# Combining expert outputs: gathered rows against an accumulating scatter into the residual in DRAM

## The chip, the cores and the metric

One core of a Trainium2 chip (trn2) runs the whole program. The metric is the device time of one execution in microseconds; the time of a kernel is the median over its runs.

## The reference

The input `x` is 4 x 512 tokens of width 256. Four sublayers are added to it in turn, each scaled by the tanh of a gate:

1. an attention-free block with a banded position bias (`_aft_local`) and a feed-forward part,
2. a mixture of experts: eight experts with two 256 x 256 matrices and a squared relu between them, beside a shared expert of width 512; each token goes to its best two of eight,
3. slot attention with a GRU cell, three iterations,
4. a mixture of experts with gate, up and down matrices (256 x 512, 512 x 256) and biases, again two of eight.

For both mixtures the part that matters here is

```python
# first:  out[token] += weight * expert_e(x[token]) for the two chosen e
binned = jnp.zeros((E, cap, Cc), x.dtype).at[sorted_e, local_pos].set(x[sorted_tok])
inter = jnp.square(jax.nn.relu(jnp.einsum('ecd,efd->ecf', binned, w1_stack)))
outb = jnp.einsum('ecf,edf->ecd', inter, w2_stack)
flat_out = outb[sorted_e, local_pos] * sorted_w[:, None]
moe_out = jnp.zeros((t, Cc), x.dtype).at[sorted_tok].add(flat_out)
# second: y = sum_e probs[n, e] * ((silu(x g_e + gb_e) * (x u_e + ub_e)) d_e + db_e)
y = jnp.einsum('ne,ned->nd', probs, expert_out)
```

## The kernel before, in words

All five engines run a program of their own; semaphores order them. The work has four parts. **A** (the first block, the shared expert and the first routing) and **C** (slot attention and the second routing) run over four batches of 512 tokens in pairs; in which order each engine takes their stages is written out by hand in `ORDER_A` and `ORDER_C`. Behind each stands an **expert loop**, `moe_*(…, m)` with m = 0 and 1, and behind that a **combination**.

*Routing.* `choose` picks two experts for each token and the two factors (`share`), `place` a row for each in the table `routed` in DRAM, and `scatter` (GpSimd, L770) writes the normalised rows there by indirect DMA, eight issues per batch of 512 tokens. `table_dve` turns the counts into a table: which groups of 256 rows belong to which expert, and where they begin. `fill` (L394, on SP) writes zero rows behind the last row of each expert: three ahead of the first group (`first_group_in`, L399), five behind its load. `table_dve` ends with the source row of every token in `outputs` (L633 to L644).

*Expert loop.* For each expert e, each engine reads its first and last group from the table (`bounds`) and loops over them, 19 groups in the first and 21 in the second part. For group t: SP loads `xg` two groups ahead (L392); TensorE turns it (L554), ScalarE copies the high halves `xt` (L469), DVE subtracts to get the low halves (L502). A product of two f32r pairs is three matmuls (L194 to L196), called `product`. TensorE makes the up products, 12 or 48 matmuls, turns the group after next, and makes the down products into two banks, 12 or 24 matmuls. ScalarE and DVE work between them on parts of 128 hidden units. DVE evicts the result to `y` (L540, or L542 with the bias), and SP stores it to `outputs` (L429).

*Weights of the experts.* `raw` is one buffer, `split` two. SP loads the plain weights of the next expert to `raw` (`raw_in`, L374). GpSimd loads the high halves by a casting DMA once expert e - 2 is done (`weights_hi`, L441), and subtracts to get the low halves (`weights_lo`, L449). The first low halves of the second part are DVE's. The attention weights of part C are loaded by SP in the loop of expert 2 (`attention_weights`), with casting loads by GpSimd (L454).

*Combination.* GpSimd waits until all of `y` has landed (`moe_end`) and gathers two rows for each token from `outputs` (L830), eight indirect DMAs per batch. DVE's `combine` (L1266) adds them with their factors to the residual, eight instructions per batch. Behind the first loop, in part C, the first pair of batches is combined before its slots are normalised and the second pair in the first iteration of the first; GpSimd makes the low halves of the GRU weights (L853, L854) behind the first two gathers. Behind the second loop all four batches are combined one after the other, and SP stores them to `out` (L732).

## Time and profile before

| | us |
|---|---|
| median of 3 runs | 1438.11 (1436.95 to 1443.64) |
| the profiled execution | 1434.66 |
| its span, first to last instruction | 1432.9 |
| TensorE busy in it | 1089.3 (76%) |
| DVE busy | 751.5 (52%) |
| ScalarE busy | 387.9 (27%) |
| GpSimd busy | 365.4 (26%) |
| bytes moved | 114.66 MB |

The profile is one execution; its time lies 3.45 us under the median. Engines are called PE (TensorE), PEld (its weight loads), DVE, ACT (ScalarE), POOL (GpSimd) and SP (SyncE, which only issues DMAs). Busy time is no bound by itself here, since the four parts follow one another and each has a different engine in front. Part A lasts until about 400 us, the first expert loop until 524, part C until about 1154, the second loop until 1380.

### The profile page before, as it was taken

How to read it: one execution, taken by the hardware profiler on the slowest of the kernel's cores; microseconds unless marked ns; L12 is line 12 of the kernel's file. 1: busy time of each engine (PE TensorE's matmuls, PEld its weight loads, DVE VectorE, ACT ScalarE, POOL GpSimd, SP SyncE). 2: the span in 40 equal slices, each digit the busy share in tenths (PEclk: the TensorE clock that was granted, in tenths of full speed). 3: DMA queues.
4: the chain of work that ended last, by engine and by line, in shares of the span. 5: the costliest groups of instructions: out<-in, count | busy, mean ns of one | idle time of the engine just before them, and what ended most of it. 6: DMA issues, size and time to landing. Idle time of an engine off the chain costs nothing.

```text
span 1432.9 us, 16450 instructions
## 1 busy us (share of the span) xinstructions
PE 1089.3 (76%) x5562; PEld 896.5 (63%) x5562; DVE 751.5 (52%) x1774; ACT 387.9 (27%) x705; POOL 365.4 (26%) x294
## 2 busy tenths in 40 slices
PE   1987989788756763778999857989897159999940
PEld 0646766476555653566877646868685058998840
DVE  5467555566533446455555553454535536665643
ACT  1204122031122332224242232332422023333320
POOL 4204044041411235411010132010101433224235
PEclk9999989899867896799999968989999569999975
DMA  7700023000257652100000010000000664636435
GB/s 261 240 1 30 1 66 126 1 0 0 74 163 216 179 185 65 43 16 0 1 0 0 15 52 22 0 1 1 0 1 1 196 185 141 191 111 204 145 97 169
DMA packets 92431, 114.66 MB, mean 80 GB/s; under 512 B 6608, under 2 KB 77776, under 8 KB 92240
## 3 DMA queue, kind: packets, MB, share of 16 engines
q1 hardware_dynamic: 72480, 78.46, 16.8%
q0 software_dynamic: 19888, 35.40, 8.6%
q8 instruction: 34, 0.56, 0.2%
q14 instruction: 29, 0.24, 0.1%
HBM read 77.14 MB, written 36.70 MB: 79 GB/s over the span
## 4 chain that ended last, share of the span: by engine, by line
PE 46%; issue 18%; DVE 15%; POOL 5%; DMA 5%; ACT 5%; SPq 3%; another core or an unknown queue 0%; DVEq 0%; POOLq 0%; ACTq 0%
PE PS L194 11%; PE PS L196 10%; PE PS L195 10%; PE PS L1586 7%; DMA xg<-routed 3%; PE PS L1502 2%; POOL routed L770 2%; POOL HB L830 2%; PE PS L1477 1%; POOL rstd L763 1%; DVE SM L1319 1%; PE PS L1398 1%; PE PS L1569 1%; PE PS L1525 1%; ACT HB L992 1%
## 5 line engine op out<-in xcount | busy, mean ns | idle before, releaser
L763 POOL TENSOR_TENSOR rstd<-ve,minus_half 128x4 f32<-128x4 f32 x40 | 40.6, 1016 | 411.9 <-DVE ve L1052 251.2
L194 PE MATMUL PS<-xt,split 128*128 128x256 f32 x412 | 123.4, 300 | 15.4 <-issue 12.3
L195 PE MATMUL PS<-xt,split 128*128 128x256 f32 x412 | 121.4, 295 | 0.0
L196 PE MATMUL PS<-xt,split 128*128 128x256 f32 x412 | 121.2, 294 | 0.0
L1586 PE MATMUL PS<-VP,HB 128*128 128x257 f32 x384 | 98.9, 422 | 15.6 <-DVE VP L1331 15.6
L1586 PEld LDWEIGHTS PS<-VP,HB 128*128 128x128 f32 x384 | 81.7, 214 | 34.6 <-DVE VP L1331 20.6
L449 POOL TENSOR_TENSOR split<-raw,split 128x1024 fp32r<-128x1024 f32 (+1 forms) x15 | 66.6, 4442 | 141.7 <-DMA raw<-down_w 74.2
L194 PEld LDWEIGHTS PS<-xt,split 128*128 128x128 f32 x412 | 84.4, 205 | 19.1 <-issue 15.2
L770 POOL DMA_INDIRECT routed<-S,dest x64 | 65.5, 1024 | 100.1 <-DVE dest L1123 82.9
L194 PE MATMUL PS<-split,hs 128*128 128x256 f32 x244 | 79.2, 324 | 11.6 <-DVE hs L509 10.1
L195 PEld LDWEIGHTS PS<-xt,split 128*128 128x128 f32 x412 | 84.3, 205 | 0.0
L196 PEld LDWEIGHTS PS<-xt,split 128*128 128x128 f32 x412 | 84.1, 204 | 0.0
L830 POOL DMA_INDIRECT HB<-outputs,source x64 | 64.6, 1009 | 66.0 <-DMA outputs<-y 47.3
L488 ACT ACTIVATE act<-PS,colv 128x256 f32<-128x256 f32 x84 | 39.8, 474 | 129.2 <-PE PS L196 129.2
L195 PE MATMUL PS<-split,hs 128*128 128x256 f32 x244 | 71.1, 291 | 0.0
L196 PE MATMUL PS<-split,hs 128*128 128x256 f32 x244 | 71.0, 291 | 0.0
L554 PE MATMUL PS<-ident,xg 128*128 128x128 f32 x168 | 28.0, 293 | 55.9 <-DMA xg<-routed 55.9
L524 DVE SCALAR_TENSOR_TENSOR act<-PS,colv,act 128x256 f32<-128x256 f32 x84 | 40.6, 484 | 52.4 <-ACT act L488 48.2
L194 PE MATMUL PS<-HTS,WHH 128*128 128x512 f32 x144 | 61.4, 426 | 8.9 <-DVE RT L1060 8.9
L1398 PE MATMUL PS<-ident,S 128*128 128x128 f32 x208 | 31.3, 300 | 45.7 <-DVE S L1056 45.5
L992 ACT ACTIVATE HB<-PS,SM 128x512 f32<-128x512 f32 x48 | 33.0, 687 | 117.1 <-DVE SM L1321 106.4
L194 PEld LDWEIGHTS PS<-split,hs 128*128 128x128 f32 x244 | 48.1, 197 | 22.2 <-DVE hs L509 22.0
(305 smaller groups left out, 2811.6 us busy)
## 6 DMA issues: line engine op xcount, KB each, us to landing
xg<-routed SPq DMA_DIRECT2D x44, 256.0 KB, 2.8
outputs<-y SPq DMA_DIRECT2D x40, 256.0 KB, 3.0
outputs<-zeros SPq DMA_DIRECT2D x3, 2048.0 KB, 16.1
routed<-zeros SPq DMA_DIRECT2D x20, 256.0 KB, 5.1
raw<-m_w SPq DMA_DIRECT2D x16, 256.0 KB, 5.6
split<-m_w POOLq DMA_DIRECT2D x16, 256.0 KB, 4.4
x_base<-X SPq DMA_DIRECT2D x8, 512.0 KB
raw<-gate_w SPq DMA_DIRECT2D x8, 512.0 KB, 7.4
```

Source lines behind the costliest of these rows:

```text
L194: pe.matmul(out_, a[1], b[0], start=first, stop=False)
L195: pe.matmul(out_, a[0], b[1], start=False, stop=False)
L196: return pe.matmul(out_, a[0], b[0], start=False, stop=last)
L449: eng.tensor_tensor(w.split[e % 2][:, 1], w.raw[:], w.split[e % 2][:, 0].bitcast(F32), ALU.subtract).then_inc(sem(f"m{m}_lo"), 1)
L488: act.activation(w.act[:, f % 2, 0], PS[:, f, 0:G], ACT.Sigmoid, bias=col("gate_b", b)).then_inc(sem(f"m{m}_act"), 1)
L524: dve.scalar_tensor_tensor(out=a[:, 1], in0=PS[:, f, 0:G], scalar=col("gate_b", e * w.fc + f), in1=a[:, 0], op0=ALU.add, op1=ALU.mult).the ...
L763: pool.tensor_tensor(rstd[h][:], ve[h][:], minus_half[:], ALU.pow).then_inc(sem("rstd_ready"), 1)
L770: pool.indirect_dma_start(out=routed[m], out_offset=bass.IndirectOffsetOnAxis(ap=dest[m][:, n, j, kk:kk + 1], axis=0), in_=S2[h][:, j], in ...
L830: pool.indirect_dma_start(out=rows_h[h][:, kk, j], out_offset=None, in_=outputs, in_offset=bass.IndirectOffsetOnAxis(ap=source[:, n, j, kk ...
L992: act.activation(HB[h][:, j], bank(h, j), ACT.Exp, bias=SM[h][:, 1, j:j + 1], scale=1.0 / 16, accum_out=SM[h][:, 2, j:j + 1]).then_inc(sem ...
L1398: ins = pe.transpose(bank(h, k + c)[:, j * P:(j + 1) * P], src[:, j, c * P:(c + 1) * P], ident[:])
L1586: ins = pe.matmul(bank(h, j)[:, 0:D + 1], HB[h][:, m, j * P:(j + 1) * P], VP[h][:, m, 0:D + 1], start=m == 0, stop=m == TT - 1)
```

## The change

- **Rows carry their own target.** A row of `routed` grows from 256 to 265 floats: the token's number and eight factors, zero except for its two experts. `choose` writes them behind the normalised row in `S2` (now `rows_of`), at the price of two more small DVE instructions per batch. `fill` writes rows that point past the tokens, with factors of zero.
- **Expert outputs are added in DRAM.** ScalarE takes the last nine columns of `xg` aside (`keep`, `shift`: two 128x18 copies per group). The eviction multiplies by the factor: in the first loop DVE does it for each half of 128 rows (`y_out`), in the second DVE adds the bias and ScalarE scales both halves in place (`y_biased`, `y_scaled`). GpSimd then casts the 128 row numbers (`to_row`) and issues an indirect DMA with an add (`add_rows`). In the first loop the two halves go to different tensors, `x_base[0]` and a zeroed `x_add`, each with a semaphore of its own. In the second loop both go to `x_base[1]`, and the second half is issued when the first has landed. `y` stays one buffer.
- **No gathers, no `outputs`.** The three zero fills of 2 MB become one, for `x_add`. Part C loads residual and `x_add` and adds them in one DVE instruction per batch. Behind the second loop SP copies `x_base[1]` to `out`, DRAM to DRAM, in four DMAs. `table_dve` loses the source rows.
- **Weights.** `raw` is two buffers (the second lies in `S0` or `HB`), and SP loads two experts ahead. The high halves are made by ScalarE from `raw` (`weights_hi`), except for the first two experts of the first loop. The low halves are DVE's in the first loop and stay GpSimd's in the second.
- **Places.** Two fills stay ahead of the first group, six go to ScalarE's DMA queue (`late_fills`). The attention weights are loaded behind the second `xg` of the first loop, and GpSimd's casting loads of them ahead of the loop.

```diff
-        routed = [nc.dram_tensor(f"routed{m}", (XROWS, D), F32, kind="Internal").ap() for m in range(2)]
-        outputs = nc.dram_tensor("outputs", (NG * G, D), F32, kind="Internal").ap()
+        x_base = [nc.dram_tensor(f"x_base{m}", (B * T + P, D), F32, kind="Internal").ap() for m in range(2)]
+
+        x_add = nc.dram_tensor("x_add", (B * T + P, D), F32, kind="Internal").ap()
+        sums = [(x_base[0], x_add), (x_base[1], x_base[1])]
...
+        def raw_buffer(m, e):
+
+            return e % 2 if m == 1 else int(e >= 2 and e % 2 == 0)
...
+            i = raw_buffer(m, e)
+            used = [f for f in range(e) if raw_buffer(m, f) == i]
+            if used:
+                sp.wait_ge(sem(f"m{m}_lo"), used[-1] + 1)
...
         def first_group_in(sp, m):
             sp.wait_ge(sem(f"m{m}_table"), 1)
-
-            for e in range(3):
-                fill(sp, m, e, "first_filled")
-            sp.wait_ge(sem("first_filled"), 48 * (m + 1))
-            sp.wait_ge(sem("filled"), 16 * (4 + m * (E - 3)))
-            sp.wait_ge(sem("outputs_filled"), 48)
+            for e in range(2):
+                fill(sp, m, e, "filled")
             for h in two:
                 sp.wait_ge(sem(f"scattered{h}"), 16 * 2 * TT * PAIRS * (m + 1))
+            sp.wait_ge(sem("filled"), 16 * (5 + 2 * (m + 1)))
             group_in(sp, m, 0)
-            for e in range(3, E):
-                fill(sp, m, e, "filled")
-
-        def moe_sp(sp, m, more):
-            w = moe[m]
+
+        def late_fills(act, m):
+            for e in range(2, E):
+                fill(act, m, e, "late_filled")
+
+        def moe_sp(sp, m):
             sp.wait_ge(sem(f"m{m}_turned"), 1)
+            sp.wait_ge(sem(f"m{m}_kept"), 1)
             group_in(sp, m, 1)
+            if m == 0:
+                attention_weights(sp)
+            sp.wait_ge(sem("late_filled"), 16 * (E - 2) * (m + 1))
             for e in range(E):
-                if e == 1:
-                    sp.wait_ge(sem("filled"), 16 * (4 + (m + 1) * (E - 3)))
-                if e == (2, 0)[m]:
-                    more(sp)
-                if 1 <= e < E - 1:
-                    raw_in(sp, m, e + 1)
+                if e + 2 < E:
+                    raw_in(sp, m, e + 2)
                 lo, hi = bounds(sp, m, e)
                 with sp.Fori(lo, hi) as t:
                     group_in(sp, m, t + 2)
-                    counted(sp, m)
-                    sp.wait_ge(sem(f"m{m}_y"), t + 2)
-                    sp.dma_start(outputs[bass.ds(t * G, G), :].rearrange("(a p) d -> p a d", p=P), w.y[:]).then_inc(sem(f"m{m}_yout"), 16)
...
+        def weights_hi(act, m, e, done=None):
 
             w = moe[m]
-            if e >= 2:
-
-                done = pool.value_load(table[m][0:1, e - 1:e], min_val=1, max_val=NG - 1)
-                counted(pool, m)
-                pool.wait_ge(sem(f"m{m}_down"), done)
-            for ap, at, n in expert_sources(m, e):
-                pool.dma_start(w.split[e % 2][:, 0, at:at + n].rearrange("p (c o) -> p c o", c=ap.shape[1]), ap).then_inc(sem(f"m{m}_hi{e % 2}"), 16)
+            i = raw_buffer(m, e)
+            if done is not None:
+                counted(act, m)
+                act.wait_ge(sem(f"m{m}_down"), done)
+                act.sem_inc(sem("passed"), 1)
+            act.wait_ge(sem(f"m{m}_raw{i}"), raw_loads(m, e))
+            act.activation(w.split[e % 2][:, 0], w.raw[i], ACT.Copy).then_inc(sem(f"m{m}_whi"), 1)
...
+            def add_rows(t):
+
+                pool.wait_ge(sem(f"m{m}_meta"), t + 1)
+                for a in range(G // P):
+                    pool.wait_ge(sem(f"m{m}_yout{a - a * m}"), 16 * (t + 1) if m == 0 else 32 * t + 16 + 16 * a)
+                    pool.sem_inc(sem("passed"), 1)
+                    pool.tensor_copy(to_row[:, a:a + 1], meta[:, a, 0:1]).then_inc(sem(f"m{m}_to_row"), 1)
+                    pool.wait_ge(sem(f"m{m}_to_row"), 2 * t + 2 + a)
+                    pool.wait_ge(sem(f"m{m}_y"), 2 * t + 2 + a)
+                    pool.sem_inc(sem("passed"), 1)
+                    pool.indirect_dma_start(out=sums[m][a], out_offset=bass.IndirectOffsetOnAxis(ap=to_row[:, a:a + 1], axis=0),
+                                            in_=w.y[:, a], in_offset=None, compute_op=ALU.add).then_inc(sem(f"m{m}_yout{a - a * m}"), 16)
...
+            for a in range(2 - m):
+                pool.dma_start(sums[m][a][B * T:B * T + P], pad[:, 0:D]).then_inc(sem(f"m{m}_yout{a}"), 16)
+            if m == 0:
+                attention_weights_hi(pool)
             pool.wait_ge(sem(f"m{m}_table"), 1)
-            for e in range(2, E):
-                if m == 0 and e == 3:
-                    attention_weights_hi(pool)
-                weights_hi(pool, m, e)
-                weights_lo(pool, m, e)
+            for h in two:
+                pool.wait_ge(sem(f"x_out{h}"), 16 * PAIRS * (m + 1))
+            for e in range(E):
+                if m == 1 and e < E - 1:
+                    if e == 0:
+                        pool.wait_ge(sem("m1_lo"), 1)
+                    weights_lo(pool, m, e + 1)
+                lo, hi = bounds(pool, m, e)
+                with pool.Fori(lo, hi) as t:
+                    counted(pool, m)
+                    add_rows(t)
+            moe_end(pool, m, hi)
...
+            def y_scaled(t, e):
+
+                act.wait_ge(sem("m1_biased"), t + 2)
+                act.wait_ge(sem("m1_meta"), t + 1)
+                for a in range(G // P):
+                    act.activation(w.y[:, a], w.y[:, a], ACT.Copy, scale=meta[:, a, 1 + e:2 + e]).then_inc(sem(f"m{m}_y"), 1)
...
+                if 1 - m <= e < E - 1:
+                    weights_hi(act, m, e + 1, lo if e else None)
...
+                    else:
+                        x_hi(t + 2)
                         h_hi(t, w.fc - 1)
+                        shift(t)
+                        keep(t + 2)
+                        y_scaled(t, e)
...
+            def y_out(t, e):
+
+                dve.wait_ge(sem(f"m{m}_down"), t + 1)
+                dve.wait_ge(sem(f"m{m}_meta"), t + 1)
+                for a in range(G // P):
+                    dve.wait_ge(sem(f"m{m}_yout{a}"), 16 * t + 16)
+                    dve.tensor_scalar(w.y[:, a], PS[:, 5 + a, 0:D], meta[:, a, 1 + e:2 + e], None, ALU.mult).then_inc(sem(f"m{m}_y"), 1)
+
+            def y_biased(t, e):
+
+                dve.wait_ge(sem(f"m{m}_down"), t + 1)
+                dve.wait_ge(sem(f"m{m}_yout0"), 32 * t + 16)
+                dve.tensor_tensor(w.y[:], PS[:, 5:7, 0:D], DB[:, e].unsqueeze(1).to_broadcast([P, G // P, D]),
+                                  ALU.add).then_inc(sem(f"m{m}_biased"), 1)
...
-            def combine(m, n, h):
-
-                x_t = residual(n, h) if m == 0 else X[h]
-                if m == 0 and n >= 2:
-                    dve.wait_ge(sem(f"second_in{h}"), 32)
+            def combine(n, h):
+
+                if n < 2:
+                    dve.wait_ge(sem(f"x_in{h}"), 16 * (PAIRS + 2))
                 else:
-                    dve.wait_ge(sem(f"x_in{h}"), 16 * (PAIRS + 1) + (m and 16 * (n // 2 + 1)))
-                dve.wait_ge(sem(f"rows{h}"), 16 * 2 * TT * (m * PAIRS + n // 2 + 1))
-                for kk in range(2):
-                    for j in range(TT):
-                        ins = dve.scalar_tensor_tensor(out=x_t[:, j], in0=rows_h[h][:, kk, j], scalar=share[m][:, n, j, kk:kk + 1],
-                                                       in1=x_t[:, j], op0=ALU.mult, op1=ALU.add)
-                        if kk == 1 and j == TT - 1:
-                            ins.then_inc(sem("combined"), 1)
-                        elif j == TT - 1:
-                            step(ins)
-                            chained()
+                    dve.wait_ge(sem(f"second_in{h}"), 48)
+                x_t = residual(n, h)
+                dve.tensor_tensor(x_t[:], x_t[:], added[n], ALU.add).then_inc(sem("combined"), 1)
 
...
+            late_fills(act, 0)
...
-            moe_sp(sp, 1, lambda sp: raw_in(sp, 1, 1))
-            for pair in range(PAIRS):
-                for n, h in of_pair[pair]:
-                    if pair:
-                        sp.wait_ge(sem(f"x_out{h}"), 16 * (2 * PAIRS + pair))
-                    sp.dma_start(X[h][:], x_base[1, n].rearrange("(j p) d -> p j d", p=P)).then_inc(sem(f"x_in{h}"), 16)
-                for n, h in of_pair[pair]:
-                    sp.wait_ge(sem("combined"), B + n + 1)
-                    sp.dma_start(out[n].rearrange("(j p) d -> p j d", p=P), X[h][:]).then_inc(sem(f"x_out{h}"), 16)
+            moe_sp(sp, 1)
+            for n in range(B):
+                sp.dma_start(out[n], x_base[1][n * T:(n + 1) * T]).then_inc(sem(f"x_out{n % 2}"), 16)
             for h in two:
                 sp.wait_ge(sem(f"x_out{h}"), 16 * 3 * PAIRS)
```

Three places in the order of the instructions. First GpSimd in the second expert loop, at a change of expert, before (`raw` and `split` are weights, rows of `ISA` and registers are small):

```order
L437 ISA x2
L441 DMA split<-gate_w 128x2x512 [waits m1_down,m1_table]
L441 DMA split<-up_w 128x2x512
L441 DMA split<-down_w 128x4x256
L449 TENSOR_TENSOR split<-raw,split 128x3072 [waits m1_raw,m1_hi0]
```

and now:

```order
L473 TENSOR_TENSOR split<-HB,split 128x3072 [waits m1_lo,x_out1,m1_whi,x_out0,m1_table]
L360 TENSOR_LOAD table
L360 ISA x2
L361 TENSOR_LOAD table
L361 ISA x2
L509 UNCONDITIONAL_BRANCH
L485 REGISTER_ALU [waits m1_table]
L487 ISA [waits m1_meta]
L489 CAST to_row<-meta 128x1 [waits m1_yout0]
L490 ISA
L493 DMA x_base<-y,to_row 2176x256 [waits m1_to_row,m1_y]
```

GpSimd had only the weights of each expert; it now stands in every group, behind the same subtraction. Second, ScalarE in the second loop, from the end of a group over a change of expert to the next group's first sigmoid, now:

```order
L524 ACTIVATE hs<-PS 128x256 [waits m1_h]
L534 REGISTER_ALU
L535 ISA [waits m1_kept]
L537 ACTIVATE meta<-meta_next 128x18 [waits m1_to_row,m1_y]
L527 REGISTER_ALU
L530 ACTIVATE meta_next<-xg 128x18 [waits m1_meta,m1_xg]
L544 ACTIVATE y<-y,meta 128x256 [waits m1_meta,m1_biased]
L544 ACTIVATE y<-y,meta 128x256
...
L462 ACTIVATE split<-raw 128x3072 [waits m1_table,m1_down,m1_raw0]
...
L561 ACTIVATE act<-PS,colv 128x256 [waits m1_up]
```

Before, the sigmoid (L488) followed directly on the copy of `hs` (L474). Third, SP at the very end, before:

```order
L729 DMA X<-x_base 128x4x256 [waits m1_yout]
L729 DMA X<-x_base 128x4x256
L732 DMA out<-X 128x4x256 [waits combined] x2
L729 DMA X<-x_base 128x4x256 [waits x_out0]
L729 DMA X<-x_base 128x4x256 [waits x_out1]
L732 DMA out<-X 128x4x256 [waits combined] x2
```

and now:

```order
L811 DMA out<-x_base 16x8192 [waits m1_yout0]
L811 DMA out<-x_base 16x8192 x3
```

Four copies that wait for the last add alone stand where eight transfers waited for DVE.

## Rows read from the trace of the kernel before

**Rows 1.** The page: the span.

```profile
span 1432.9 us, 16450 instructions
```

**Rows 2.** Order of time behind the second loop (start us, us, engine, line, operation).

```profile
1383.15 1.04 POOL L830 DMA_INDIRECT HB<-outputs,source  x1 [33.83 <-DMA outputs<-y]
...
1423.02 0.95 POOL L830 DMA_INDIRECT HB<-outputs,source  x1 [0.30 <-issue]
...
1426.11 3.38 DVE L1266 SCALAR_TENSOR_TENSOR X<-HB,share,X 128x256 f32<-128x256 f32 x8 [4.68 <-DMA HB<-outputs,source]
...
1421.46 8.43 SPq L732 DMA_DIRECT2D out<-X  x2
```

**Rows 3.** Busy time of each engine in the second expert loop.

```profile
1160.90:1379.20 218.30, 207.23 (x1600) 197.69 (x1600) 136.33 (x295) 78.52 (x192) 60.94 (x25) 0.97 0.48 149
```

**Rows 4.** Order of time at the start of the second loop.

```profile
1145.88 3.35 DVE L449 TENSOR_TENSOR split<-raw,split 128x3072 fp32r<-128x3072 f32 x1
1146.59 3.46 POOL L770 DMA_INDIRECT routed<-S,dest  x1 [0.30 <-issue]
1150.36 0.96 POOL L770 DMA_INDIRECT routed<-S,dest  x1 [0.30 <-issue]
1153.60 0.40 SPq L392 DMA_DIRECT2D xg<-routed  x1
...
1160.92 1.09 PE L554 MATMUL PS<-ident,xg 128*128 128x128 f32 x4 [22.03 <-DMA xg<-routed]
```

**Rows 5.** DVE's evictions in the second loop, in order of time.

```profile
1176.11 0.69 DVE L542 TENSOR_TENSOR y<-PS,DB 128x512 f32<-128x512 f32 x1 [1.18 <-PE PS L196]
1185.70 0.69 DVE L542 TENSOR_TENSOR y<-PS,DB 128x512 f32<-128x512 f32 x1 [1.17 <-PE PS L196]
1196.31 0.69 DVE L542 TENSOR_TENSOR y<-PS,DB 128x512 f32<-128x512 f32 x1 [1.17 <-PE PS L196]
...
1379.20 0.69 DVE L542 TENSOR_TENSOR y<-PS,DB 128x512 f32<-128x512 f32 x1 [1.17 <-PE PS L196]
```

**Rows 6.** Groups by line in the second loop (busy us, mean ns of one).

```profile
L449 POOL TENSOR_TENSOR split<-raw,split 128x3072 fp32r<-128x3072 f32 x7 | 47.7, 6821 | 85.7 <-DMA raw<-down_w 74.2 <-DMA split<-down_w 11.5
...
L527 DVE SCALAR_TENSOR_TENSOR PS<-PS,colv,act 128x256 f32<-128x256 f32 x80 | 39.4, 493 | 2.9
...
L509 DVE TENSOR_TENSOR hs<-PS,hs 128x256 fp32r<-128x256 f32 x80 | 33.1, 414 | 0.0
```

**Rows 7.** Order of time in the first loop: transposes and evictions.

```profile
410.19 1.12 PE L554 MATMUL PS<-ident,xg 128*128 128x128 f32 x4 [4.31 <-DMA xg<-routed]
...
414.00 0.69 DVE L540 COPY y<-PS 128x512 f32<-128x512 f32 x1 [1.34 <-PE PS L196]
...
418.97 0.69 DVE L540 COPY y<-PS 128x512 f32<-128x512 f32 x1 [0.97 <-PE PS L196]
...
444.65 0.69 DVE L540 COPY y<-PS 128x512 f32<-128x512 f32 x1 [1.87 <-PE PS L196]
457.30 0.69 DVE L540 COPY y<-PS 128x512 f32<-128x512 f32 x1 [1.34 <-PE PS L196]
...
524.24 0.69 DVE L540 COPY y<-PS 128x512 f32<-128x512 f32 x1 [0.97 <-PE PS L196]
```

**Rows 8.** ScalarE's copies from SBUF by line (ns min/median/max, first and last start).

```profile
L889 ACT ACTIVATE W<-HB x1: 1482/1482/1482, 11.4 to 11.4; 128x1536 fp32r<-128x1536 f32 x1
...
L485 ACT ACTIVATE hs<-act x38: 416/417/418, 405.1 to 521.6; 128x256 fp32r<-128x256 f32 x38
```

**Rows 9.** Order of time behind the first loop.

```profile
548.24 10.44 DVE L1266 SCALAR_TENSOR_TENSOR X<-HB,share,X 128x256 f32<-128x256 f32 x8
...
553.78 3.42 POOL L854 TENSOR_TENSOR WHH<-HB,WHH 128x1536 fp32r<-128x1536 f32 x1
...
563.42 1.94 PE L1398 MATMUL PS<-ident,S 128*128 128x128 f32 x8 [16.09 <-DVE S L1056]
...
620.05 6.67 DVE L1266 SCALAR_TENSOR_TENSOR XN<-HB,share,XN 128x256 f32<-128x256 f32 x16
```

**Rows 10.** The page: one kind of DMA issue (count, KB each, us to landing).

```profile
outputs<-zeros SPq DMA_DIRECT2D x3, 2048.0 KB, 16.1
```

216 lines of the change are left out of this document (107 added, 109 removed), and 4 rows, old and new, of the table ORDER_C.

## The prediction

> **What bounds the kernel now.** I read the page first, then the two expert loops in order of time, then the stretches behind each of them. The span is 1432.9 us in a run of 1434.66 [rows 1]; no engine bounds it as a whole, so each stage has to be read by itself. The places that the change touches are these.
>
> *Behind the second expert loop (53.7 us).* The last eviction into `y` starts at 1379.20 [rows 5], and everything up to the end, 1432.9, is the combination: the store of `y` has to land, GpSimd issues 32 gathers one behind the other from 1383.15 to 1423.97, DVE starts on the last batch at 1426.11, and its store ends the span [rows 2]. TensorE has nothing to do there. Look at the gap between 1423.97 and 1426.11: 2.14 us from the end of an issue to its reader.
>
> *In the second expert loop (203 us).* From the first `y` to the last there are 20 intervals, 1379.20 - 1176.11 = 203.1 [rows 5]. Within an expert one takes 9.59 us, across a change of expert 10.61. TensorE is busy in 207.2 of the 218.3 us from its first transpose at 1160.92 on, at a granted clock of 0.97 [rows 3]: this stage is bound by TensorE, and the rest follows in its shadow.
>
> *In the first expert loop (110 us).* 18 intervals from 414.00 to 524.24; a good one is 4.97, the one ahead of 457.30 is 12.65 [rows 7]. Here the chain TensorE, ScalarE, DVE decides, and twice a DMA. The second group's transposes also waited 4.31 us for their `xg` [rows 7].
>
> *Behind the first loop.* DVE's combination of two batches is one after the other in its queue: the first piece takes 10.44 us, because one of its instructions stands still while GpSimd subtracts the GRU weights at 553.78, and TensorE waits 16.09 us for what follows [rows 9].
>
> **The part that no row shows: how long an accumulating scatter takes to land.** Call L the time from the end of GpSimd's issue to the reader. The nearest rows: a gather, 2.14 [rows 2]; a plain scatter, ended 1151.32 and followed by its reader at 1153.60, so at most 2.28 [rows 4]. An accumulate must read the old row in DRAM before it writes, so neither is an upper end. I take 3.0, which is the scatter and a third more, since 128 rows are a small transfer and what is added is mostly one more trip; for the bounds I take 2.3 (the read costs nothing) and 4.4 (the gather and the scatter one after the other). The Trainium skill (DMA: Bandwidth & Descriptors, section "Anatomy of one DMA — SWDGE (gpsimd) path") fits a DMA from GpSimd by 2.0 us and its bytes over 436 GB/s, which for 128 KB would be an estimate of 2.3; by that, the sum below would be about 1406. No run here shows yet that an accumulate obeys this fit, and the same skill (Collectives: The Full Stack, section "The bandwidth ceiling: the fold count and why AG ≠ RS ≠ AR") says that an add costs two source reads, which speaks against it.
>
> **The change part by part**, against 1434.66.
>
> 1. *The end.* 32 gathers, four combinations and their stores go. In their place, from the last eviction: 0.69 for the bias (as the old eviction, [rows 5]), 0.42 for ScalarE's scaling of one half (the 128x256 row, [rows 8]), two issues of 0.96 [rows 4], and about 0.8 for the small cast and six handovers (estimated from the 0.3 between neighbouring issues); that is 3.8, and L twice, since in this loop the second half's add waits for the first's. With L = 3 it is 9.8. Then the copy of 2 MB from DRAM to DRAM. The nearest row is a 2 MB store, 16.1 us in a queue of three [rows 10]; alone it should take less, but bytes are both read and written. I take 12 and half a microsecond for its issue; bounds 8 and 20. 9.8 + 12.5 = 22.3 in place of 53.7: **-31** (-36 to -22).
>
> 2. *Second loop, new experts.* The high halves are now made by ScalarE in 128x3072. From 0.417 us at 256 and 1.482 at 1536 [rows 8], a column costs 0.83 ns, so 2.8 us. For six experts this copy waits until the group before has left TensorE, and what is queued behind it on ScalarE is the first sigmoid of the new expert. That sigmoid was due some 2.5 us after the last matmul (12 matmuls of 207.2 / 1600 = 0.13, [rows 3], and the 1.0 by which a change of expert is longer); it now comes at 1.8 (bias and scaling) + 2.8 = 4.6. The sigmoid takes some 0.5, DVE has then 4 x (2 x 0.49 + 0.41) + 0.7, about 6.3 with no pause [rows 5, 6], and TensorE's last six matmuls of 0.13 stand behind it: 12.2 us against 10.61, so 1.6 x 6 = 10, and 2 for the first group and for ScalarE's scaling in each. **+12** (0 if DVE's pauses take it up, 19 if all 2.8 count).
>
> 3. *Second loop, the adds.* A group's adds are a chain of their own: 3.8 + 2L = 9.8 per group, and `y` can't be overwritten before it has ended. GpSimd also makes the low halves, 6.82 us each [rows 6], ahead of the new expert's adds, which I put at 2 more per change. 20 x 9.8 + 12 = 208 is under TensorE's own 203 + 12 = 215, so at L = 3 it costs **0**. The cover is 7 us, and it is gone at L = 3.2: from there each 0.1 of L costs 4 us.
>
> 4. *Start of the second loop.* `xg` was issued at 1153.60 and read at 1160.92, 7.3 us, since fills, casts and the next weights were in flight [rows 4]. Now the late fills leave from ScalarE before, and the casts are gone; the scatters ahead stay, and so does the 3.46 us one beside DVE's 3.35 us subtraction. **-4** (-6 to 0).
>
> 5. *First loop.* The second `xg` is asked for at once, not behind five fills and two stores: -5. But the attention weights (2.25 MB) and their casting loads (1.75 MB), formerly in the middle, now stand ahead of the third `xg`: +6. The stalls that they and the store of `y` made in the middle go: -10.5, of which 7 in the interval of 12.65 [rows 7]. Two halves go to two tensors, so only one landing counts: issue, cast, issue, landing and eviction again, about 1.75 + L = 4.75 for the second half, under 4.97, but the second half is late by a microsecond and DVE stands behind it: 0.5 x 11 = +5.5. ScalarE's and DVE's copies of 128x1024 at six changes: 0.8 each, +5. **+1** (-10 to +15). DVE's subtraction reads two SBUF tensors while GpSimd issues; rows 4 show what that does to an issue, 3.46 in place of 0.96, and I count at most 1.2 us at a change, hidden by its length. The Trainium skill (SBUF — State Buffer, "Who interferes with whom") infers that such an op does not hold up descriptor generation; by it this would be nothing, and the row says otherwise.
>
> 6. *Behind the first loop.* The second halves' add must land, where a plain store was: **+3**. DVE's combination is one addition of 128x1024 per batch, some 1.2 us (a third of the 3.35, [rows 4], and a little that is fixed), and GpSimd's subtractions come long before it: 9 us on the first batch and 2 on the second, less 1 for the extra loads: **-10** (-12 to -4). In the second pair 6.67 us of combination [rows 9] become 2.5 beside TensorE's gates: **-1**.
>
> 7. Six MB of zeros at the start become two: nothing waits for them, **0**. The routing's extra DVE instructions: **0**.
>
> Sum: -31 + 12 + 0 - 4 + 1 + 3 - 10 - 1 = **-30**, 1404.7 for the profiled execution. The median of the three runs is 3.45 above it, so I forecast **1408 us**. A measurement can tell about 0.5%, 7.2 us, from no change.
>
> **The rivals.**
>
> *The adds take over the second loop (slower).* Place: `y` of one group waits for both adds of the group before, one behind the other. At L = 4.2 a group costs 12.2: 20 x 12.2 + 12 - 203 = +53 in place of +12, with 12 more at the end and in the first loop: -30 + 41 + 12 = +23, **1461**. It decides from L = 3.8, where gains and losses cancel. For it: nothing shows L, the chain takes it 42 times in all, and 9.8 against 10.1 is a thin cover. Against: no plain transfer of this size needs over 2.3. Chance 0.18; between L = 3.7 and 3.9 it is no change, 0.1.
>
> *Copies and adds both in the shadow (faster still).* L = 2.3, and DVE's pauses (1.2 us ahead of each eviction, [rows 5]) take up ScalarE's copy: 8 less in the second loop, 5 in the first, 6 at the end: **1389**. For it: TensorE alone is full. Chance 0.12.
>
> *Transfers crowd the start of the first loop.* 8 MB between 392 and 425 push several `xg`, 15 us in place of 6, and routed rows of 1060 bytes land more slowly: **1423**. Chance 0.1. That the change does not do what it says I leave out: the order of instructions shows the gathers gone.
>
> **How the numbers follow.** The forecast (L up to 3.4: 1395 to 1420) has 0.5. Faster: 0.5 + 0.12 + 0.1 = 0.72; same 0.1; slower 0.18. The range goes from the second rival, a little beyond, to L = 4.05 of the first: 1386 to 1452, with some 0.06 left out below and 0.13 above.
>
> **What would show it.** Right: the stretch behind the last eviction near 22 us; intervals of the second loop 9.6 within an expert and 12 across; TensorE's wait behind the first loop near 7 us, not 16. Wrong: evictions in the second loop that wait for a DMA into `x_base` (then L is over 3.2, and the row gives it), intervals that are alike within and across experts, or an end over 30 us, which would be the DRAM copy.

## The result, and the profile after

The changed kernel takes **1460.65 us** (median of 4 runs, 1460.25 to 1464.78) where the kernel before took 1437.63 (4 runs, 1436.95 to 1443.64): a ratio of 1.019, 95% interval 1.016 to 1.023. It is slower by 23 us, where 1408 was forecast. That is nearly the value of the first rival (1461). The rival had the right place, but it got there with L = 4.2 in every group, and most landings took 2.1 to 3.0 us; that its figure fits is in part luck.

From the page of the changed kernel, which answers to [rows 1]: the span, the chain of waits by engine and by line, and two groups of instructions (busy, mean ns | idle before and who ended it).

```profile
span 1459.0 us, 17260 instructions
...
PE 42%; DMA 18%; DVE 18%; issue 9%; POOL 6%; ACT 5%; SPq 1%; DVEq 1%; POOLq 1%; ACTq 0%
...
L201 PE MATMUL PS<-split,hs 128*128 128x256 f32 x244 | 86.0, 352 | 85.7 <-DVE hs L589 85.1
L493 POOL DMA_INDIRECT x_base<-y,to_row x61 | 95.7, 1569 | 99.3 <-DVE y L597 45.9
```

DMA has 18% of the chain, and 12% of the span lies in it as `x_base<-y,to_row`, the landing of an add. An add's issue takes GpSimd 1569 ns; the plain scatter of [rows 4] takes 960. TensorE stands still for 85.7 us ahead of its down products.

I cut both profiled executions by the same points: VectorE's first subtraction into `xt` of each loop, the start of the last group's eviction into `y` in each loop (its first half, where it has two), and the end. The cuts of the kernel before are 402.20, 524.24, 1162.83, 1379.20 and 1432.9, those of the changed kernel 408.71, 550.63, 1171.01, 1438.39 and 1459.0.

| stage | before | changed | difference | forecast |
|---|---|---|---|---|
| part A, up to the first loop | 402.2 | 408.7 | +6.5 | 0 |
| first loop | 122.0 | 141.9 | +19.9 | +1 |
| part C, to the second loop | 638.6 | 620.4 | -18.2 | -12 |
| second loop | 216.4 | 267.4 | +51.0 | +12 |
| end | 53.7 | 20.6 | -33.1 | -31 |

Their sum is +26.1, the difference of the spans. Where the forecast counted on a gain it came, larger than stated. The loss lies in the two loops, and 6.5 us in part A (term 7 below).

The second loop of the changed kernel in the windows (us, then busy time and count of PE, PEld, DVE, ACT and POOL, granted clock, DMA share, GB/s), which answers to [rows 3]:

```profile
1171.01:1438.39 267.38, 218.60 (x1596) 207.23 (x1596) 132.16 (x295) 121.21 (x280) 117.57 (x87) 0.91 0.36 78
```

TensorE was busy in 207 of 218 us [rows 3]; now it is in 219 of 267, and no longer sets the pace of the loop. Who holds it shows in one group inside an expert, from one eviction to the next, in the timeline of the changed kernel (start, us, engine, line; idle before and who ended it), VectorE, ScalarE and GpSimd in turn:

```profile
1297.89 0.69 DVE L603 TENSOR_TENSOR y<-PS,DB 128x512 f32<-128x512 f32 x1 [4.00 <-DMA x_base<-y,to_row]
...
1309.22 0.69 DVE L603 TENSOR_TENSOR y<-PS,DB 128x512 f32<-128x512 f32 x1 [3.64 <-DMA x_base<-y,to_row]
```
```profile
1298.62 0.91 ACT L544 ACTIVATE y<-y,meta 128x256 f32<-128x256 f32 x2 [4.95 <-DVE y L603]
```
```profile
1298.03 0.19 POOL L489 CAST to_row<-meta 128x1 int32<-128x1 f32 x1 [2.60 <-DMA x_base<-y,to_row]
1299.91 1.56 POOL L493 DMA_INDIRECT x_base<-y,to_row  x1 [1.70 <-ACT y L544]
1303.71 0.19 POOL L489 CAST to_row<-meta 128x1 int32<-128x1 f32 x1 [2.24 <-DMA x_base<-y,to_row]
1305.01 1.56 POOL L493 DMA_INDIRECT x_base<-y,to_row  x1 [1.11 <-issue]
```

Read it as a sum. Eviction and the first half's scaling to 1299.08; 0.83 until GpSimd issues; 1.56 of issue, ended 1301.47; landing at 1303.71, 2.24 later; cast 0.19; 1.11 until the next issue; 1.56, ended 1306.57; and the next eviction starts at 1309.22, 2.65 later. Together 11.33 us, with no slack anywhere, against the 9.59 of TensorE [rows 5]. Both landings together are 4.89, so L was 2.45 here; the rest is 6.44, where my sum had 3.8. This is the shortest interval but the first: the 20 of them take 255.1 us, 12.8 on average.

Two things make the others longer. Ahead of the first add of a new expert GpSimd subtracts low halves for 6.8 to 7.4 us. Here VectorE had written `y` at 1206.91, and the add was issued 6.17 us later, where the group above has 2.02; the next eviction came 15.11 us after the one before:

```profile
1204.24 7.41 POOL L473 TENSOR_TENSOR split<-raw,split 128x3072 fp32r<-128x3072 f32 x1
1210.99 0.78 POOL L489 CAST to_row<-meta 128x1 int32<-128x1 f32 x1
1213.08 1.56 POOL L493 DMA_INDIRECT x_base<-y,to_row  x1 [1.31 <-issue]
```

And some landings stretch. This one was in flight when SyncE issued the next expert's 1.5 MB (1343.77 to 1345.2); the cast that waits for it follows 7.02 us behind the issue's end:

```profile
1343.12 1.56 POOL L493 DMA_INDIRECT x_base<-y,to_row  x1 [0.81 <-POOL to_row L489]
1351.70 0.19 POOL L489 CAST to_row<-meta 128x1 int32<-128x1 f32 x1 [7.02 <-DMA x_base<-y,to_row]
```

Most landings in this loop took 2.1 to 3.0 us; six took 3.7 to 6.9 (the one above to VectorE), and five of these six lay beside or up to 3.6 us behind an issue of an expert's weights.

In the first loop GpSimd passes from one half to the next with little pause in places, and VectorE's second half waits for the landing of the add before:

```profile
460.58 1.56 POOL L493 DMA_INDIRECT x_base<-y,to_row  x1 [0.82 <-POOL to_row L489]
462.27 0.19 POOL L489 CAST to_row<-meta 128x1 int32<-128x1 f32 x1
463.39 1.57 POOL L493 DMA_INDIRECT x_add<-y,to_row  x1 [0.94 <-DVE y L597]
```
```profile
470.56 0.48 DVE L597 TENSOR_SCALAR y<-PS,meta 128x256 f32<-128x256 f32 x1 [4.50 <-DMA x_add<-y,to_row]
```

The end, which answers to [rows 2]: the last cast, the last issue, and SyncE's copy to the output behind the landing.

```profile
1444.31 0.19 POOL L489 CAST to_row<-meta 128x1 int32<-128x1 f32 x1 [2.33 <-DMA x_base<-y,to_row]
1445.37 1.57 POOL L493 DMA_INDIRECT x_base<-y,to_row  x1 [0.87 <-POOL to_row L489]
```
```profile
1449.18 2.52 SPq L811 DMA_DIRECT2D out<-x_base  x4
```

From the last eviction to 1449.18 there are 10.8 us, and from there to the end, 1459.0, the 2 MB from DRAM to DRAM take 9.8.

Behind the first loop TensorE's longest wait for VectorE's combination is 6.75 us, where it was 16.09 [rows 9]; this sign of the forecast came true:

```profile
587.74 1.94 PE L1444 MATMUL PS<-ident,S 128*128 128x128 f32 x8 [6.75 <-DVE S L1112]
```

### The profile page after: what moved, and what is told of

Same layout as the page of the kernel before. It is cut to its first block, busy times and chain, and to the rows that moved or that the text cites. A ratio compares the mean times of both kernels' runs of the same rounds, so it can differ in the third digit from the quotient of the medians.

```text
span 1459.0 us, 17260 instructions
## 1 busy us (share of the span) xinstructions
PE 1101.1 (75%) x5562; PEld 908.3 (62%) x5562; DVE 728.3 (50%) x1737; ACT 449.0 (31%) x843; POOL 401.3 (28%) x354
## 4 chain that ended last, share of the span: by engine, by line
PE 42%; DMA 18%; DVE 18%; issue 9%; POOL 6%; ACT 5%; SPq 1%; DVEq 1%; POOLq 1%; ACTq 0%
DMA x_base<-y,to_row 12%; PE PS L201 8%; PE PS L203 7%; PE PS L202 7%; PE PS L1632 6%; PE PS L1548 4%; DMA x_add<-y,to_row 3%; PE PS L1523 3%; POOL routed L853 2%; POOL rstd L846 2%; PE PS L1444 2%; PE PS L1571 1%; DVE st L1101 1%; DVE SM L1368 1%; DMA xg<-routed 1%
## 5 line engine op out<-in xcount | busy, mean ns | idle before, releaser
L201 PE MATMUL PS<-split,hs 128*128 128x256 f32 x244 | 86.0, 352 | 85.7 <-DVE hs L589 85.1
L201 PE MATMUL PS<-xt,split 128*128 128x256 f32 x412 | 122.5, 297 | 11.1 <-issue 8.0
L493 POOL DMA_INDIRECT x_base<-y,to_row x61 | 95.7, 1569 | 99.3 <-DVE y L597 45.9
L201 PEld LDWEIGHTS PS<-split,hs 128*128 128x128 f32 x244 | 55.4, 227 | 99.4 <-issue 50.0
L1632 PE MATMUL PS<-VP,HB 128*128 128x257 f32 x384 | 94.9, 410 | 15.7 <-DVE VP L1380 15.7
L1632 PEld LDWEIGHTS PS<-VP,HB 128*128 128x128 f32 x384 | 78.8, 207 | 33.5 <-DVE VP L1380 20.6
L201 PEld LDWEIGHTS PS<-xt,split 128*128 128x128 f32 x412 | 82.9, 201 | 14.7 <-issue 10.9
L203 PEld LDWEIGHTS PS<-xt,split 128*128 128x128 f32 x412 | 82.4, 200 | 0.0
L202 PEld LDWEIGHTS PS<-xt,split 128*128 128x128 f32 x412 | 82.2, 200 | 0.0
L202 PE MATMUL PS<-split,hs 128*128 128x256 f32 x244 | 77.7, 318 | 0.0
L203 PE MATMUL PS<-split,hs 128*128 128x256 f32 x244 | 77.4, 317 | 0.0
L489 POOL CAST to_row<-meta 128x1 int32<-128x1 f32 x80 | 28.2, 352 | 128.6 <-DMA x_base<-y,to_row 102.5
L201 PE MATMUL PS<-RT,W 128*128 128x512 f32 x96 | 42.0, 438 | 25.4 <-DVE RT L1281 17.2
```

The lines of the kernel that those rows point to most:

```text
L201: pe.matmul(out_, a[1], b[0], start=first, stop=False)
L202: pe.matmul(out_, a[0], b[1], start=False, stop=False)
L203: return pe.matmul(out_, a[0], b[0], start=False, stop=last)
L493: pool.indirect_dma_start(out=sums[m][a], out_offset=bass.IndirectOffsetOnAxis(ap=to_row[:, a:a + 1], axis=0), in_=w.y[:, a], in_offset=No ...
L1632: ins = pe.matmul(bank(h, j)[:, 0:D + 1], HB[h][:, m, j * P:(j + 1) * P], VP[h][:, m, 0:D + 1], start=m == 0, stop=m == TT - 1)
```

## The experiments

Theory A: the adds' own chain holds both loops. Theory B: the weights' new way (ScalarE's copy, GpSimd's subtraction, 1.5 MB in flight) does. All kernels start from the changed one unless said. The stages of all of them by the same cuts, in us of their profiled executions, with the times (no adds, plain stores, early cast and the first "attention weights later" are single runs). Beside these kernels the kernel before took 1433.2 to 1438.1 us; ratios are to the one beside each, and a few us between two rows of the last column say nothing:

| kernel | A | first loop | C | second loop | end | time |
|---|---|---|---|---|---|---|
| before | 402.2 | 122.0 | 638.6 | 216.4 | 53.7 | 1437.6 |
| changed | 408.7 | 141.9 | 620.4 | 267.4 | 20.6 | 1460.7 |
| no adds | 404.5 | 100.9 | 620.1 | 221.5 | 13.5 | 1362.1 |
| plain stores (20 groups in the second loop) | 408.9 | 122.0 | 623.5 | 228.7 | 18.4 | 1403.1 |
| early cast | 404.8 | 140.4 | 625.3 | 257.4 | 20.4 | 1450.1 |
| attention weights later | 408.1 | 139.8 | 625.6 | 270.1 | 20.9 | 1466.3 |
| two arrays | 409.9 | 140.3 | 625.7 | 221.8 | 27.8 | 1424.1 |
| one array, no wait | 403.1 | 140.5 | 626.3 | 222.1 | 16.9 | 1413.3 |
| row per choice | 406.2 | 121.4 | 622.5 | 221.9 | 28.3 | 1403.4 |
| same, attention later | 410.6 | 121.8 | 621.5 | 221.9 | 28.2 | 1402.8 |
| same, copy shared | 411.6 | 124.6 | 622.1 | 214.1 | 28.0 | 1396.9 |
| same, casts by VectorE | 406.1 | 116.0 | 620.9 | 214.3 | 28.2 | 1393.5 |

**No adds**, and no waits for a landing:

```
-                    pool.wait_ge(sem(f"m{m}_yout{a - a * m}"), 16 * (t + 1) if m == 0 else 32 * t + 16 + 16 * a)
-                    pool.indirect_dma_start(out=sums[m][a], ..., compute_op=ALU.add).then_inc(...)
-                dve.wait_ge(sem(f"m{m}_yout0"), 32 * t + 16)
+                dve.wait_ge(sem(f"m{m}_y"), 2 * t + 1)
```

> Both loops without the indirect adds (the products are computed, scaled and thrown away; nothing waits for a landing); the weights' part of the change stays. Known by now: with the halves of the second loop in two arrays its intervals fell to 9.6 us inside an expert and about 12.2 at a change of expert, 209.5 us for 20 of them; the first loop stayed at 136 us. Theory A, that only the adds cost the first loop its 25 us: its 18 intervals fall from 134.9 to 110 to 115 us, the second loop to 203 to 212 us. Theory B, that the weights' new way costs part: the first loop stays at 120 us or more.

The second loop fell from 267.4 to 221.5, its 20 intervals to 208.8, in theory A's range; the first from 141.9 to 100.9, its 18 intervals to 93.8, well under both ranges. So theory B explains none of the 20 us of the first loop (without stores of any kind it is 21 us shorter than before, and with plain stores, below, as long as before), and 5 us of the second, where intervals across experts are 12.1 in place of 10.6. Look at TensorE in the two windows:

```profile
404.45:505.34 100.89, 73.86 (x532) 67.66 (x532) 64.12 (x139) 50.39 (x140) 6.79 (x37) 0.94 0.37 108
1125.42:1346.87 221.45, 207.16 (x1596) 195.14 (x1596) 134.40 (x295) 120.34 (x280) 54.68 (x48) 0.99 0.23 69
```

The same 532 instructions of the first loop are busy for 73.9 us at a granted clock of 0.94, where the changed kernel has 87.0 at 0.82.

**Plain stores**, the sum left out:

```
-                                            in_=w.y[:, a], in_offset=None, compute_op=ALU.add).then_inc(...)
+                                            in_=w.y[:, a], in_offset=None).then_inc(...)
```

> The same indirect stores without the accumulation (they overwrite the rows, so the sum is left out). If accumulation is what makes the issue long: issue 0.96 us in place of 1.57, hand-over 0.3 us in place of 0.8, so up to 2.2 us less per group in the second loop, which falls from 255 to about 215 to 230 us. If the length comes from something else (two sources, the wide destination, the other engines): issue stays at 1.5 us or more, the loop at 250 to 258 us. Landing: theory A says 2.2 to 2.4 us either way; if the read of the old row costs, the plain store lands 0.5 us or more sooner.

1403.1 us in one run, but of less work: with the sums left out the second routing comes out otherwise, and the second loop has 20 groups (1520 matmuls) in place of 21 (1596). One group more would be some 10 us, by the intervals of 9.6 (an estimate). Both things got shorter, the issue and the landing, in GpSimd's timeline of the second loop:

```profile
1364.84 0.98 POOL L493 DMA_INDIRECT x_base<-y,to_row  x1 [3.20 <-ACT y L544]
1367.44 0.19 POOL L489 CAST to_row<-meta 128x1 int32<-128x1 f32 x1 [1.61 <-DMA x_base<-y,to_row]
1368.44 0.98 POOL L493 DMA_INDIRECT x_base<-y,to_row  x1 [0.82 <-POOL to_row L489]
```

0.98 in place of 1.57, and 1.61 in place of 2.24 to 2.5. The hand-over of 0.82 behind the cast stayed, so I was wrong to expect it to shrink. Accumulating costs 1.3 us a DMA, 2.6 a group where two stand in series, which takes 11.33 to 8.7 (an estimate), under TensorE's 9.6; four of the last five intervals are 9.6. But VectorE still waits for landings in six groups, 23.5 us in all (66.8 in 15 groups with the adds), and intervals of up to 15.4 us remain around the changes of expert. In the first loop, which has its 532 matmuls in both kernels, leaving accumulation out gives 19.9 us, 1.05 per group, close to the two issues' 1.2.

**Two arrays in the second loop**, so that the halves don't wait for each other; both row numbers are cast at once, and at the end both arrays are loaded and summed:

```
-        sums = [(x_base[0], x_add), (x_base[1], x_base[1])]
+        sums = [(x_base[0], x_add), (x_base[1], x_add1)]
...
+                pool.tensor_copy(to_row[:], meta[:, :, 0]).then_inc(sem(f"m{m}_to_row"), 2)
```

> In the second loop the halves of a group go to two arrays, as in the first loop, so the second add no longer waits for the landing of the first; at the end both arrays are loaded, summed by VectorE and stored. Theory A: the chain of a group falls from 10.8 us (6.2 + 2 x 2.3) to about 8.2 us, under the 9.6 us of TensorE; intervals inside an expert 9.6 to 9.9 us in place of 11.3, the 20 intervals 215 to 228 us in place of 255; the end 28 to 32 us in place of 20.6; time about 1430 to 1445 us. Theory B: the intervals at changes of expert stay at 12 to 15 us, the loop at 240 us or more, and with the longer end the time is 1455 us or more.

1424.09 us, ratio to before 0.9925 (0.990 to 0.995); intervals 9.6 inside an expert, 12.1 to 12.4 across, 209.5 for 20, end 27.8. That is theory A, and better than its ranges: 215 to 228 for the 20 intervals, 1430 to 1445 for the time. The loop is back at what it is without any adds (221.8 against 221.5), and VectorE waits for no landing in it. So the wait of the second half for the first half's landing, with the cast and the hand-over behind it, is what makes the adds cost 46 us (the early cast alone, below, gives back 10). The landings beside weights in flight and GpSimd's subtraction are here too, and cost nothing once the chain is short; they took part in the 46 only through it.

**Early cast**: in the second loop both row numbers are cast ahead of the first add.

```
+                    pool.tensor_copy(to_row[:], meta[:, :, 0]).then_inc(sem("m1_to_row"), 2)
...
+                    if m == 0 or a == 1:
+                        pool.wait_ge(sem(f"m{m}_yout{a - a * m}"), ...)
```

> Second loop: both row numbers of a group are cast at once before its first add, so the second add needs nothing but the landing of the first. The trace of the changed kernel shows 0.19 us of cast and 0.81 us of hand-over between that landing and the second issue, a term that my sum had only once per group. If the cast and its hand-over are what stands there, the second issue comes 0.1 to 0.3 us behind the landing: 0.7 to 0.9 us less per group, the 20 intervals 255 us to 237 to 243 us. If GpSimd needs 0.8 us behind any wait before it can issue, only the cast's 0.2 us goes: 250 us or more.

The 20 intervals came to 245.0, between the two expectations. GpSimd does need its 0.8 behind the wait for the landing: issue ended 1260.43, next one 1263.54, 3.11 later, which is 2.3 (the landing, by the changed kernel's casts) and 0.8.

```profile
1258.88 1.55 POOL L500 DMA_INDIRECT x_base<-y,to_row  x1 [1.64 <-ACT y L551]
1263.54 1.55 POOL L500 DMA_INDIRECT x_base<-y,to_row  x1 [3.11 <-DMA x_base<-y,to_row]
```

So a hand-over behind each landing is a term by itself, with or without a cast. From the end of one issue to the next the changed kernel has 3.3 to 3.5 us in most groups, so leaving out the cast gave back 0.2 to 0.4 in each, 4 to 8 us of the 10. The intervals are 11.2 to 14.5 in place of 11.3 to 17.7 (the first left out), and 3.8 us of the gain lie at the two longest; what made those shorter I can't tell.

**Attention weights later**, back ahead of the third expert:

```
-            if m == 0:
-                attention_weights(sp)
...
+                if m == 0 and e == 2:
+                    attention_weights(sp)
```

> The loads of the attention weights go back to where they stood before (ahead of the loads at the third expert) in place of the start of the first loop. In the changed kernel the first interval of the first loop is 10.4 us. If the loads at the start crowd the third group of rows out: that interval falls to 5.5 to 7 us and the first loop's 18 intervals from 134.9 to 129 to 132 us. If the adds are the bound of the loop anyway, or the loads stretch landings just as much later on: 134 to 137 us.

The crowding was real, and taking it away gained 2 us of the loop and nothing of the time (1466.3 in one run). In the changed kernel TensorE waits 5.31 us for the third group of rows; here that wait is 0.23, and the loop takes 139.8 in place of 141.9. The edit was tried again on a kernel without accumulation (below).

```profile
422.29 1.12 PE L646 MATMUL PS<-ident,xg 128*128 128x128 f32 x4 [5.31 <-DMA xg<-routed]
```

**One array, no wait.** In a group only padding rows of the two halves can coincide; they get numbers of their own, and both adds go to the one array back to back:

```
-                    pool.wait_ge(sem(f"m{m}_yout{a - a * m}"), ... 32 * t + 16 + 16 * a)
+                    pool.wait_ge(sem("m1_yout0"), 32 * t + 16)
...
+                pool.iota(pad[:, at:at + 1], pattern=[[0, 1]], base=B * T + a * P, channel_multiplier=1, ...)
```

> Accumulation kept, and in the second loop both halves of a group are added to the one array without waiting between them: only their padding rows could coincide, and these get row numbers of their own. Theory A: chain of a group 8 to 8.5 us, under TensorE's 9.6; intervals 9.6 us inside an expert and about 12.1 at a change, 20 of them 208 to 212 us, and the end stays at 20 to 22 us: time 1413 to 1421 us, 7 us less than with two arrays. Rival: two accumulating stores in flight in one array slow each other (landing 3.5 us or more), and the loop stays at 220 us or more.

1413.28 us, ratio 0.989 (0.983 to 0.994). As with two arrays, both row numbers are cast at once. The loop is as short as there (222.1, 20 intervals 208.9), and the end is 16.9, shorter than the 20 to 22 expected:

```profile
1299.13 1.55 POOL L499 DMA_INDIRECT x_base<-y,to_row  x1 [3.49 <-ACT y L551]
1300.99 1.55 POOL L499 DMA_INDIRECT x_base<-y,to_row  x1 [0.30 <-issue]
```

0.30 between two issues with nothing to wait for, and behind the last issue of the loop (ended 1397.51) the copy starts at 1399.82, 2.31 later: two adds in flight in one array don't slow each other. This is the smallest repair tried here that makes the change pay, by 1.1%.

**Row per choice.** No accumulation. Each token has two experts, so each result is stored plainly to a row (token, first or second choice), and the sums are made on VectorE (the main lines of the edit):

```
-                                            in_=w.y[:, a], in_offset=None, compute_op=ALU.add).then_inc(...)
+                                            in_=w.y[:, a], in_offset=None).then_inc(...)
...
+                step(dve.scalar_tensor_tensor(out=rows_of[h][:, :, D:D + E], in0=R[:, 5], scalar=float(B * T),
+                                              in1=token[:, n]..., op0=ALU.mult, op1=ALU.add))
```

> No accumulation at all: every token has two experts, so a group's rows are stored by plain indirect DMA to a row of their own (token, first or second choice), and part C and the end load both rows of each token and VectorE sums them. From the run with plain stores (issue 0.98 us, landing 1.63 us behind it, first loop 114.8 us) and the run with two arrays (second loop 209.5 us, end 27.8 us, 1424.1 us): first loop 113 to 117 us, second loop 206 to 211 us (no landing is waited for between the halves), four more sums of 1.2 us in part C and at the end: +2 to +8 us. Time 1400 to 1414 us. The rival, that more loads (two arrays of 2 MB behind each loop) cost what the adds saved: 1420 us or more.

1403.39 us, ratio 0.979 (0.975 to 0.983). First loop 121.4 (18 intervals 114.1), second 221.9 with 208.7 for 20 intervals, part C as long as in the other kernels, end 28.3. All as expected.

**The same, attention weights later.**

> The kernel with a row per choice, with the loads of the attention weights back ahead of the third expert. In the kernel with the adds this edit took the first interval of the first loop from 10.4 to 5.3 us and gave nothing back in time (135.7 us for the loop). If that was so because the adds bound the loop anyway, the edit now pays: first loop 114.1 us to 108 to 111 us, time 3 to 5 us under the 1403.4 us of the run without it, 1396 to 1402 us. If the crowding only moves to another place of the loop: 112 to 116 us and no change in time.

1402.83 us, ratio 0.979 (0.975 to 0.982); first loop 121.8. The wait for the third group's rows fell from 5.68 to 0.37 us, and again nothing came of it. My first explanation, that the adds hid the gain, falls; VectorE waits 14.6 us for landings in both kernels, and why the loop isn't shorter stays open.

**The same, copy shared**: VectorE copies half of the high halves in the second loop.

```
+            part = slice(0, w.cols // 2 if m == 1 and e else w.cols)
+            act.activation(w.split[e % 2][:, 0, part], w.raw[i][:, part], ACT.Copy).then_inc(...)
...
+            dve.tensor_copy(w.split[e % 2][:, 0, part], w.raw[i][:, part]).then_inc(sem("m1_whi"), 1)
```

> The same, and in the second loop ScalarE copies only half of an expert's high halves (128x1536 in place of 128x3072), VectorE the other half. An interval with a change of expert is 12.1 us with ScalarE's copy of 2.8 us ahead of its next sigmoid, 10.6 us before the change. If that copy is the 1.5 us of difference: 10.6 to 11.2 us at the seven changes, the 20 intervals 208.7 us to 200 to 204 us, and the start of the loop 1 us shorter. If VectorE's copy now stands in the way instead, or GpSimd's subtraction is the bound there: 206 us or more.

1396.88 us, ratio 0.974 (0.971 to 0.977). Intervals across experts 10.8 to 11.1, the 20 together 200.9. Half of ScalarE's copy, 1.3 us of 2.8, gave back 1.3 of the 1.5 us at each of six changes, so the copy was the cause. The start of the loop, 13.2 us to its first eviction, didn't get shorter, against the expectation. In the timeline (ScalarE, then VectorE) VectorE's half is over before ScalarE's:

```profile
1214.05 1.49 ACT L479 ACTIVATE split<-HB 128x1536 fp32r<-128x1536 f32 x1 [0.44 <-issue]
```
```profile
1213.55 0.96 DVE L491 CAST split<-HB 128x1536 fp32r<-128x1536 f32 x1 [0.88 <-issue]
```

**The same, casts by VectorE** in the first loop:

```
-                    pool.tensor_copy(to_row[:, a:a + 1], meta[:, a, e:e + 1]).then_inc(...)
+                    dve.tensor_copy(to_row[:, a:a + 1], meta[:, a, e:e + 1]).then_inc(...)
```

> The last kernel, with the casts of the row numbers of the first loop taken from GpSimd to VectorE, ahead of each half of its eviction. From the start of the loop to its last eviction this stage took 141.9 us with the adds, 122.0 and 121.4 us with plain stores and 100.9 us with none: per group GpSimd spends 2 x (1.57 + 0.8 + 0.2) = 5.1 us with adds and 2 x (0.98 + 1.0) = 4.0 us without accumulation, and the steps between these kernels are 1.05 and 1.1 us per group. If GpSimd's own row of cast, hand-over and issue is what holds this loop, about 1 us per group goes: 104 to 112 us, time 1382 to 1390 us. If the landing of the stores (1.6 us) and the wait of VectorE for it hold it: 118 us or more, and 1395 us or more.

1393.46 us, ratio 0.973 (0.969 to 0.976), the lowest median of those that compute the whole, but the runs (1384.98 to 1400.01) overlap those with the copy shared (1394.71 to 1402.30), so a gain in time over that kernel isn't shown. First loop 116.0, time 1393: both between the two expectations. GpSimd's two issues are now 0.30 apart (465.14 and 466.40), so its row of work is down to about 3 us per group, and 5 to 9 us of the loop went with it (121.4 to 124.6 in the three kernels with a row per choice ahead of it). The profiled run is a quick one (1387.29), and that of the kernel ahead a slow one (1402.30), so the upper end is doubtful. The other 15 us above the loop without stores are VectorE's waits for landings (7.3 us in the loop) and what I haven't separated.

## Why the prediction was wrong

- **Term 1, the end (-31): right**, -33.1. The adds took 10.8 (forecast 9.8), the copy from DRAM to DRAM 9.8 (forecast 12.5).
- **Term 2, ScalarE's copy (+12): mechanism right, sum too large.** Per change 1.5 us against 1.6 forecast, shown by sharing the copy. With the adds out of the way the loop is 5 to 6 us longer than before, not 12: the kernel before has one interval of 14.5 us (1304.90 to 1319.40) at a change of expert, where these have 12.1, and of the 2 us for the first group and the scaling 0.7 came.
- **Term 3, the second loop's adds (0): this is the step that failed.** It measured +46 (267.4 against 221.8 with the halves separated). What failed first is the fixed part of 3.8 per group and not L, on which the text spent its care: L was 2.45 in the quiet group above, and 2.1 to 3.0 in most, where 3.0 was assumed. The fixed part is 6.44. The issue was taken from a plain scatter's row, 0.96, and an accumulating one takes 1.57 (twice: +1.2); the "small cast and six handovers" at 0.8 were estimated from the 0.3 between neighbouring issues, which is the gap when nothing is waited for, and are 0.83 behind ScalarE and 0.19 + 1.11 behind the first landing (+1.3). Issue and landing together, 0.96 + 3.0 = 3.96, would have been near the 1.57 + 2.3 = 3.87 measured; the hand-over behind a landing, left out, took the cover. At a change of expert TensorE itself takes 12.1, so 11.3 against 9.6 counts in the 13 intervals inside an expert alone: 13 x 1.7 = 22 us, an estimate. The other half is what one figure for L and "2 more per change" hid. Six landings of 3.7 to 6.9 us are 13 us above 2.5, and the first add of a new expert was issued 1 to 4 us late behind GpSimd's subtraction in six groups, 12 us in all; each of them falls on a chain without slack. By subtraction the intervals inside an expert have 41 of the 46 us, those across a change 4.
- The same step named the cover as 7 us, gone from L = 3.2, which is 0.4 us more per group. That figure alone said that the forecast hung on a guess, and a chance of 0.18 for the rival was too low: the bounds were put on L only, and none on the fixed part.
- **Term 4, start of the second loop (-4), and term 6 (+3, -10, -1): the sum about right, the parts not all.** Part C with the start came to -18.2 in the changed kernel's profile and -12 to -18 in the ten other kernels with this part C or nearly this; -12 was forecast. TensorE's wait behind the loop fell as said, to 6.75 us. In term 4 the first `xg` was read 2.9 us behind its issue, not 7.3, as forecast; but it was issued 5.5 us behind the end of the last scatter (1160.82), where it had been 2.3. By the profile SyncE waited for that scatter's landing, with ScalarE's six fills and two of its own on their way, so only 1.3 us of the 4 came:

```profile
1154.88 7.45 ACTq L418 DMA_DIRECT2D routed<-pad  x6
1159.85 0.96 POOL L853 DMA_INDIRECT routed<-S,dest  x1 [0.31 <-issue]
1166.28 0.40 SPq L413 DMA_DIRECT2D xg<-routed  x1
1169.15 1.09 PE L646 MATMUL PS<-ident,xg 128*128 128x128 f32 x4 [20.44 <-DMA xg<-routed]
```

Some 6 us of part C's gain lie later in the part, behind TensorE's first product with `WHH` (634.07), where nothing was forecast; what they are wasn't looked into. The 3.46 us issue of [rows 4] came back as 3.17 beside VectorE's subtraction of 3.34:

```profile
1155.10 3.17 POOL L853 DMA_INDIRECT routed<-S,dest  x1 [0.30 <-issue]
```

- **Term 5, the first loop (+1): two errors that partly cancel.** Without any store the loop is 21 us shorter than before (100.9 against 122.0; the loop before had its stores), where the parts of my sum other than the adds, -5 + 6 - 10.5 + 5, made -4.5. The adds cost +41, of which plain stores are 21 and accumulation 20; I had +5.5. I followed one half's chain (4.75 us, under 4.97) and not GpSimd's own row, 2 x (1.57 + 0.81 + 0.19) = 5.1 us for a group, with no room for any wait; taking the casts out of that row gave 5 us or more. VectorE's waits for landings go the same way: 29.9 us in the changed loop, 13.0 with plain stores, 7.3 in the last kernel, none without adds. How the 41 us divide between the two isn't shown, nor what the clock adds (13 us more of TensorE's busy time, at 0.82 for 0.94). The +6 for the crowded third `xg` was measured as 5.31, not the 15 of the third rival, and was worth 2 us at most.
- **Term 7 (0): open.** Part A took 408.7 in place of 402.2; the other changed kernels have 403.1 to 411.6 with the same code, those without the 2 MB of zeros among them, so the zeros are not the reason. What is, if it isn't the spread from run to run, wasn't tried.
- Of the signs named in advance, the one against the forecast appeared: evictions in the second loop that wait for a DMA into `x_base`. Its reading, "then L is over 3.2", was wrong too, since the fixed part can do the same. The second sign against it, intervals alike within and across experts, appeared as well: 10.9 to 17.7 and 12.0 to 13.1 us.

Two estimates from the Trainium skill can now be held against rows. DMA: Bandwidth & Descriptors (section "Anatomy of one DMA — SWDGE (gpsimd) path") gives 2.3 us for 128 KB, setup and completion included, and I had set that against L alone. With GpSimd's issue counted the accumulating store takes 1.56 + 2.24 = 3.8 us and the plain one 0.98 + 1.61 = 2.6; the second is near the estimate, the first is not. So that L alone is near 2.3 with the add doesn't bear the estimate out. SBUF — State Buffer ("Who interferes with whom") infers that an operation with two SBUF operands doesn't hold up descriptor generation; the 3.17 us above, an issue that also reads its row numbers from SBUF, speaks against it a second time.

## What to carry to other kernels

When a step becomes a chain of DMA, wait, DMA, price each link from a row of the same kind of link: the issue of that very form, the hand-over behind a wait and not between neighbours, the landing; then put bounds on all of them, not only on the one that looks unknown. If the chain's length comes within half a microsecond of the stage's bound, first ask whether the links must be in series at all: separating two halves that couldn't collide was worth 46 us of the loop here. And count an engine's own row of work per iteration as well as the chain through it.
